# A graph network kernel: all 79 dense node tiles counted beside the first layer's gathers, and their stores begun by ScalarE

## Chip, cores and metric

The kernel runs on one core of one Trainium2 chip. The metric is the device time of one execution in microseconds (us), lower being better. The engines are TensorE (PE, its weight loads are PEld), VectorE (DVE), ScalarE (ACT), GpSimd (POOL) and SyncE (SP). Each runs its own instructions in order, and they wait for one another through semaphores.

## What is computed

There are 12500 nodes with 64 features and 400000 edges, sorted by target `dst`; `src` is random.

```
h = relu(layernorm(x))
m = silu(LN(concat(h[src], edge_attr) @ W1 + b1))       # first layer
m = silu(m @ W2 + b2)
x = x + LN(silu(concat(segment_sum(m, dst), h) @ Wu + bu))
h = relu(layernorm(x))                                   # second layer
agg = segment_sum(h[src], dst)
x = x + relu((h + agg) @ M1 + c1) @ M2 + c2
```

## The kernel before

**First layer.** The edges are cut into 391 blocks of 1024 (8 columns of 128). For every block POOL issues 8 indirect DMAs (`gather`, L736), each fetching 128 rows of 256 bytes by `src`. The block is then pushed through a pipeline written out by hand: one *step* per block, in which every engine does its part for blocks of different age. DVE adds the gathered rows to the edge products (`z_ready`, L1128), PE transposes and multiplies, ACT applies the activations, PE sums the messages of a block into a window of 40 nodes (`window_sums`, L781), and DVE adds the window to `cT`. Gathers run up to 4 blocks ahead of DVE (`AHEAD`).

**Second layer.** Its messages are only `h[src]`, so the sum for a tile of 128 target nodes is also a dense product: a matrix of counts (128 targets by 12500 sources) times `h`, which lies in SBUF as three bf16 parts (`hparts`). A tile's product is 100 matmuls of 125x192 (`product`, L1762), followed by a copy of the sums on ACT (L1715) and a turn of 3 float32 matmuls on PE (`turn`, L1773). The edges of 76 tiles go this way; the first 92 blocks of edges are still gathered, as in the first layer but with no MLP.

**Where the counts come from.** Of the 76 tiles, 48 are *stored*: their counts are made during the first layer's steps, and go through HBM (`ctab`, 128 x 12800 bf16 = 3.28 MB a tile, 400 KB a unit). A tile is 8 *units*, and in the code before step j does one unit: DVE compares keys with numbers in PSUM (`count_hots`, L1176 and L1178), PE multiplies the one-hots in two halves (`pairs`, L984, 16 matmuls in all), ACT copies each half out of PSUM (`staged`, L1057), and SP starts the store (L934). A tile also needs one indirect DMA of its keys on POOL (L949). The other 28 tiles are *built* in the second layer itself, beside the products of the other tiles (`one_hot_pairs` L1839 and L1841 on DVE, L1783 on PE, L1723 on ACT); their keys are fetched and masked while the nodes are updated between the layers (L1415 on POOL, L1571 and L1575 on DVE). A table of slots sets that order: 8 parts for a stored tile, 16 for a built one, and a block of gathered edges every 9 parts.

The program's parts in order: setup, first layer, node update, second layer, and the final MLP over 25 batches of 500 nodes (L1896, L1904, L1912), each stage behind a barrier of all engines.

## Time and profile before

| what | value |
|---|---|
| median of 3 runs | 5619.12 us (5618.64, 5619.12, 5668.9) |
| profiled execution | 5674.2 us, span 5672.3 us |
| setup, until the first gather | 198.8 us |
| first layer, gathers | 198.8 to 4162 |
| its pipeline running empty | to 4220 |
| node update | 4221 to 4384 |
| second layer | 4387 to 5505.9 |
| final MLP | 5505.9 to 5672 |
| busy: PE, DVE, ACT, POOL | 68%, 48%, 37%, 70% |

The profiled execution is one run, 55 us above the median of the others. Busy shares are means over stages with different limits, so each stage has to be read by itself.

### The profile page before, as it was taken

How to read it: one execution, taken by the hardware profiler on the slowest of the kernel's cores; microseconds unless marked ns; L12 is line 12 of the kernel's file. 1: busy time of each engine (PE TensorE's matmuls, PEld its weight loads, DVE VectorE, ACT ScalarE, POOL GpSimd, SP SyncE). 2: the span in 40 equal slices, each digit the busy share in tenths (PEclk: the TensorE clock that was granted, in tenths of full speed). 3: DMA queues.
4: the chain of work that ended last, by engine and by line, in shares of the span. 5: the costliest groups of instructions: out<-in, count | busy, mean ns of one | idle time of the engine just before them, and what ended most of it. 6: DMA issues, size and time to landing. Idle time of an engine off the chain costs nothing. (4 is left out here: it accounts for less than half of the span.)

```text
span 5672.3 us, 77979 instructions
## 1 busy us (share of the span) xinstructions
PE 3874.2 (68%) x27143; PEld 2832.3 (50%) x27143; DVE 2750.7 (48%) x5342; ACT 2073.5 (37%) x3073; POOL 3997.2 (70%) x4016
## 2 busy tenths in 40 slices
PE   5456666666666656666666666666675989989888
PEld 4334444443444434334444443444453888888873
DVE  5445555545454545454555555555557434434331
ACT  1133333333333343334333333333333333334332
POOL 3777777777777777777777777777732777777750
PEclk9567777777787787877778777778775999999995
DMA  3122222222222222222222222222212444444431
GB/s 94 49 72 83 80 78 82 79 81 81 81 81 79 80 81 80 81 80 80 81 80 81 80 80 81 80 81 80 81 43 72 143 183 157 167 176 159 176 122 31
DMA packets 324626, 529.74 MB, mean 93 GB/s; under 512 B 153682, under 2 KB 204114, under 8 KB 317586
## 3 DMA queue, kind: packets, MB, share of 16 engines
q1 hardware_dynamic: 198162, 395.39, 19.4%
q0 software_dynamic: 126080, 129.36, 10.0%
q8 instruction: 225, 3.69, 0.3%
q14 instruction: 159, 1.30, 0.1%
HBM read 352.75 MB, written 171.69 MB: 92 GB/s over the span
## 5 line engine op out<-in xcount | busy, mean ns | idle before, releaser
L736 POOL DMA_INDIRECT gat<-layer_rows,idx x3864 | 3820.1, 989 | 1181.5 <-issue 1175.1
L1057 ACT ACTIVATE node_buffers<-ps 128x800 bf16<-128x800 f32 x768 | 642.8, 837 | 2371.4 <-PE ps L984 2371.4
L781 PE MATMUL ps<-one_hots,edge_buffers 128*128 128x80 f32 x3128 | 602.0, 355 | 1092.4 <-DVE cT L828 1092.2
L1128 DVE TENSOR_TENSOR edge_buffers<-ps,gat 128x512 f32<-128x512 f32 x391 | 270.3, 691 | 1808.7 <-issue 1532.0
L781 PEld LDWEIGHTS ps<-one_hots,edge_buffers 128*128 128x128 f32 x3128 | 541.1, 261 | 1145.9 <-issue 1135.4
L1762 PE MATMUL ps<-edge_buffers,node_buffers 125*128 125x192 bf16 x7600 | 742.5, 252 | 18.2 <-DMA node_buffers<-stored_counts 12.4
L749 PE MATMUL ps<-w1e,edge_buffers 128*128 128x256 f32 x1564 | 633.7, 547 | 107.7 <-DVE edge_buffers L1128 103.7
L1762 PEld LDWEIGHTS ps<-edge_buffers,node_buffers 125*128 125x128 bf16 x7600 | 687.8, 141 | 36.8 <-DMA node_buffers<-stored_counts 15.8
L762 PE MATMUL ps<-edge_buffers,w2d 128*128 128x512 f32 x782 | 501.4, 728 | 0.7 <-ACT node_buffers L772 0.6
L1723 ACT ACTIVATE node_buffers<-ps 125x800 bf16<-125x800 f32 x448 | 371.2, 839 | 316.6 <-PE ps L1783 292.4
L1176 DVE TENSOR_TENSOR node_buffers<-ps,node_buffers 128x1024 bf16<-128x1024 f32 x384 | 469.5, 1223 | 15.2 <-PE ps L984 5.2
L767 PE MATMUL ps<-ident,node_buffers 128*128 128x128 f32 x1564 | 285.2, 312 | 276.5 <-ACT edge_buffers L776 276.5
L749 PEld LDWEIGHTS ps<-w1e,edge_buffers 128*128 128x128 f32 x1564 | 387.8, 274 | 164.5 <-issue 110.5
L984 PEld LDWEIGHTS ps<-node_buffers 64*128 64x128 bf16 x6144 | 185.7, 106 | 557.6 <-issue 529.8
L767 PEld LDWEIGHTS ps<-ident,node_buffers 128*128 128x128 f32 x1564 | 190.4, 158 | 378.6 <-issue 378.5
L1178 DVE TENSOR_TENSOR node_buffers<-ps,node_buffers 128x800 bf16<-128x800 f32 x384 | 376.3, 980 | 0.0
L756 PE MATMUL ps<-ident,node_buffers 128*128 128x128 f32 x1564 | 331.2, 348 | 5.0 <-ACT edge_buffers L1075 4.9
L824 DVE TENSOR_TENSOR cT<-cT,ps 64x40 f32 x483 | 88.9, 184 | 480.3 <-PE ps L781 367.5
L984 PE MATMUL ps<-node_buffers 64*128 64x100 bf16 x6144 | 320.1, 234 | 0.0
L1075 ACT ACTIVATE edge_buffers<-ps,gcol 128x512 f32<-128x512 f32 x391 | 302.1, 773 | 14.0 <-PE ps L756 14.0
L772 ACT ACTIVATE node_buffers<-ps,b2col 128x512 f32<-128x512 f32 x391 | 270.4, 692 | 0.8 <-PE ps L762 0.5
L1150 DVE TENSOR_TENSOR node_buffers<-edge_buffers,ps 128x512 f32<-128x512 f32 x391 | 265.5, 679 | 3.6 <-DVE ps L294 0.3
(201 smaller groups left out, 4031.0 us busy)
## 6 DMA issues: line engine op xcount, KB each, us to landing
stored_counts<-node_buffers SPq DMA_DIRECT2D x384, 400.0 KB, 2.4
node_buffers<-stored_counts SPq DMA_DIRECT2D x48, 3200.0 KB
gat<-layer_rows,idx POOLq DMA_INDIRECT x3864
edge_buffers<-in_edge_quads SPq DMA_DIRECT2D x391, 128.0 KB, 2.0
node_buffers<-in_x SPq DMA_DIRECT2D x5, 625.0 KB
layer_rows<-node_buffers SPq DMA_DIRECT2D x25, 125.0 KB
residual_rows<-node_buffers SPq DMA_DIRECT2D x5, 625.0 KB
layer_rows<-node_buffers SPq DMA_DIRECT2D x5, 625.0 KB
```

The lines of the kernel that those rows point to most:

```text
L736: pool.indirect_dma_start(out=gat[:, j, c, :], out_offset=None, in_=table[:, :], in_offset=bass.IndirectOffsetOnAxis(ap=idx[:, half, j, c: ...
L749: mm = pe.matmul(o[:, k * 4 * F:(k + 1) * 4 * F], ea[:, j, k, :], w1e[:, :], start=True, stop=True)
L756: mm = pe.transpose(o[:, k * 128:(k + 1) * 128], zn[:, j, 2 * k:2 * k + 2, :].rearrange("p c f -> p (c f)"), ident[:, :])
L762: return pe.matmul(mp[0][:, 0:PAIRS * 128], w2d[:, :], hT[:, j, :], start=True, stop=True)
L767: mm = pe.transpose(mp[1][:, k * 128:(k + 1) * 128], msgT[:, half, k * 128:(k + 1) * 128], ident[:, :])
L781: mm = pe.matmul(to[:, 0:2 * WIN], rows_of[:, 2 * k:2 * k + 2, :].rearrange("p c f -> p (c f)"), oh[:, j, 2 * k:2 * k + 2, :].rearrange("p ...
L984: mm = pe.matmul(tp[h][:, i * T:(i + 1) * T], low_hot[node, u % 2, k, :], high_hot[node, u % 2, k, :], start=True, stop=True)
L1057: a.activation(stage[:, u % STAGES, part * GP * T:(part + 1) * GP * T].rearrange("p (i h k) -> p h i k", h=2, k=T), ps[:, 2:4, 0:4 * T].re ...
L1176: v.tensor_tensor(low_hot[:, u % 2, :, :], per_tile(low_numbers, GP), bcast(low_key[:, b % 2, at], 128), ALU.is_equal).then_inc(c_low, 1)
L1178: v.tensor_tensor(high_hot[:, u % 2, :, :], per_tile(high_numbers, GP), bcast(high_key[:, b % 2, at], T), ALU.is_equal).then_inc(c_hot, 1)
L1723: a.activation(cnt[0:TP, d % 2, ch * 8 * T:(ch + 1) * 8 * T].rearrange("p (b k) -> p b k", b=2), built[ch % 2][0:TP, :, :], ACT.Copy).then ...
L1762: mm = pe.matmul(wide[d % 2], cnt[0:TP, d % 2, t:t + (GW - 1) * T + 1:T], hparts[:, t, :, :].rearrange("p k f -> p (k f)"), start=(t == 0) ...
```

## The change

Every dense tile is now stored, 79 of them, and none is built in the second layer; 78 blocks are gathered there in place of 92. The first layer makes 13 units in 8 steps (`RATE`) instead of 8, so 5 of 8 steps hold two units. The one-hot buffers go from 2 to 4 (`PAIR_SLOTS`). ACT starts each store itself (`write_counts`), after a wait for its own two copies. In the second layer each slot is one tile and, in 78 of 79, one block; three count buffers are loaded in turn, the first while the nodes are updated.

```diff
-    STORED, BUILT = 48, 28
-    TILES = STORED + BUILT
+    TILES = 79
...
-    GB = 92
+    GB = 78
+    RATE = (13, 8)
...
-        UNITS = STORED * GPS
-        FETCH, MASK, KEYS_TURN, HOTS, COUNT, STORE = 0, 4, 6, GPS, GPS + 1, GPS + 6
+        UNITS = TILES * GPS
+        FETCH, MASK, KEYS_TURN, HOTS, COUNT = 0, 4, 6, 8, 9
+        unit_step = [u * RATE[1] // RATE[0] for u in range(UNITS)]
...
-                    u = unit_at(e, j, STORE)
-                    if u is not None:
-                        at = u % GPS * 2 * GP * T
-                        wait(sp, c_copy, 2 * u + 2)
-                        sp.dma_start(ctab[u // GPS, :, at:at + 2 * GP * T], stage[:, u % STAGES, :]).then_inc(c_st[u % STAGES], 16)
...
+                def write_counts(u):
+
+                    at = u % GPS * 2 * GP * T
+                    wait(a, c_copy, 2 * u + 2)
+                    a.dma_start(ctab[u // GPS, :, at:at + 2 * GP * T], stage[:, u % STAGES, :]).then_inc(c_st[u % STAGES], 16)
...
+                    for u in units[0:1]:
+                        write_counts(u)
+                    for u in units[1:2]:
+                        staged(u, 0)
+                        staged(u, 1)
+                        write_counts(u)
...
-                    wait(v, c_use, 2 * (u - 2) + 2)
+                    wait(v, c_use, 2 * (u - PAIR_SLOTS) + 2)
...
+        def load_counts(sp, d):
+
+            sp.dma_start(cnt[d % 3], ctab[d, :, :]).then_inc(d_load[d % 3], 16)
...
+                    for d in range(1, TILES):
+
+                        wait(sp, d_sum, d - 2)
+                        load_counts(sp, d)
...
+                    for d in range(TILES):
+                        product(d, 0, LEAD)
+                        if d > 0:
+                            turn(d - 1)
+                        product(d, LEAD, T)
+                        if d < GB:
+                            sums(d)
```

The line numbers of the code after differ a little: `window_sums` is L775, `edge_products` L743, the transposes L750 and L761, the second product L756, `product` L1668, `turn` L1679.

On PE, a step of the first layer before, from the window sums to the second half of its unit (L984):

```order
L781 MATMUL ps<-one_hots,edge_buffers 128x80 x4
L749 MATMUL ps<-w1e,edge_buffers 128x256 x2
L984 MATMUL ps<-node_buffers 128x100 x8
L756 MATMUL ps<-ident,node_buffers 128x128 x4
L767 MATMUL ps<-ident,node_buffers 128x128 x4
L762 MATMUL ps<-edge_buffers,w2d 128x512
L984 MATMUL ps<-node_buffers 128x100 x8
```

and a step that holds two units after:

```order
L775 MATMUL ps<-one_hots,edge_buffers 128x80 x4
L743 MATMUL ps<-w1e,edge_buffers 128x256 x2
L984 MATMUL ps<-node_buffers 128x100 x8
L750 MATMUL ps<-ident,node_buffers 128x128 x4
L984 MATMUL ps<-node_buffers 128x100 x8
L761 MATMUL ps<-ident,node_buffers 128x128 x4
L984 MATMUL ps<-node_buffers 128x100 x8
L756 MATMUL ps<-edge_buffers,w2d 128x512
L984 MATMUL ps<-node_buffers 128x100 x8
```

The second half moved ahead of the back transposes, and a second unit's halves lie around the second product.

On ACT, a step of the first layer before, with what each instruction waits for (activation, first copy of counts, messages, messages by feature, second copy):

```order
L1075 ACTIVATE edge_buffers<-ps,gcol 128x512 [waits l0_second_products,l0_z_transposed]
L1057 ACTIVATE node_buffers<-ps 128x2x4x100 [waits stored_counts_written1,stored_pairs_multiplied]
L776 ACTIVATE edge_buffers<-ps 128x512 [waits l0_window_summed,l0_messages_turned]
L772 ACTIVATE node_buffers<-ps,b2col 128x512 [waits l0_messages_turned,l0_second_products]
L1057 ACTIVATE node_buffers<-ps 128x2x4x100 [waits stored_counts_written1,stored_pairs_multiplied]
```

and a step with two units after:

```order
L1085 ACTIVATE edge_buffers<-ps,gcol 128x512 [waits l0_second_products,l0_z_transposed]
L1061 ACTIVATE node_buffers<-ps 128x2x4x100 [waits stored_counts_written0,stored_pairs_multiplied]
L770 ACTIVATE edge_buffers<-ps 128x512 [waits l0_window_summed,l0_messages_turned]
L1061 ACTIVATE node_buffers<-ps 128x2x4x100 [waits stored_counts_written0,stored_pairs_multiplied]
L766 ACTIVATE node_buffers<-ps,b2col 128x512 [waits l0_messages_turned,l0_second_products]
L1068 DMA stored_counts<-node_buffers 128x1600 [waits stored_counts_staged]
L1061 ACTIVATE node_buffers<-ps 128x2x4x100 [waits stored_counts_written1,stored_pairs_multiplied] x2
L1068 DMA stored_counts<-node_buffers 128x1600 [waits stored_counts_staged]
```

ACT gained two stores, each behind a wait for its own copies, and the second unit's two copies in a row.

On PE in the second layer before, where a tile is built (L1783) between pieces of another tile's product, around the window sums of a block:

```order
L1783 MATMUL ps<-node_buffers 128x200 x4
L1762 MATMUL ps<-edge_buffers,node_buffers 128x192 x8
L1783 MATMUL ps<-node_buffers 128x200 x4
L781 MATMUL ps<-one_hots,gat 128x80 x4
L1762 MATMUL ps<-edge_buffers,node_buffers 128x192 x7
```

and after, the same row of work from one slot into the next:

```order
L1668 MATMUL ps<-edge_buffers,node_buffers 128x192 x75
L775 MATMUL ps<-one_hots,gat 128x80 x4
L1668 MATMUL ps<-edge_buffers,node_buffers 128x192 x25
L1679 MATMUL ps<-ident,node_buffers 64x128 x3
L1668 MATMUL ps<-edge_buffers,node_buffers 128x192 x75
```

The pairs are gone; the product is cut once, for the turn of the tile before.

## Rows read from the trace of the kernel before

**Rows 1.** Busy time by stretch: first layer, second layer, final MLP.

```profile
core 0: us, PE busy (x) PEld busy (x) DVE busy (x) ACT busy (x) POOL busy (x), PEclk, DMA share, GB/s
1000.00:4000.00 3000.00, 1878.90 (x11386) 1226.08 (x11385) 1547.76 (x3108) 1162.16 (x1702) 2267.46 (x2404) 0.79 0.27 80
4387.00:5505.00 1118.00, 1003.91 (x10584) 960.74 (x10584) 442.05 (x800) 400.09 (x614) 868.66 (x736) 0.95 0.45 164
5540.00:5580.00 40.00, 33.83 (x94) 14.52 (x94) 5.01 (x12) 10.97 (x18) 0.00 (x0) 0.50 0.17 38
```

**Rows 2.** Waits, 1000 to 4000 us: total, times, longest.

```profile
ACT node_buffers L1057 <- PE ps L984: 1826.4, 588, 10.2
DVE edge_buffers L1128 <- issue: 1168.6, 230, 7.7
PE ps L781 <- DVE cT L828: 865.3, 262, 7.5
```

**Rows 3.** Groups of instructions, 1000 to 4000 us: count, busy, mean ns, idle before.

```profile
L736 POOL DMA_INDIRECT gat<-layer_rows,idx x2367 | 2233.3, 944 | 721.4 <-issue 721.4
L1057 ACT ACTIVATE node_buffers<-ps 128x800 bf16<-128x800 f32 x592 | 495.5, 837 | 1826.5 <-PE ps L984 1826.4
L1176 DVE TENSOR_TENSOR node_buffers<-ps,node_buffers 128x1024 bf16<-128x1024 f32 x296 | 361.9, 1223 | 9.2 <-PE ps L984 1.2 <-issue 1.0
L1178 DVE TENSOR_TENSOR node_buffers<-ps,node_buffers 128x800 bf16<-128x800 f32 x296 | 290.0, 980 | 0.0
```

**Rows 4.** Timeline of the emptying pipeline: start, duration; two steps with units, two without.

```profile
4175.45 0.97 PEld L781 LDWEIGHTS ps<-one_hots,edge_buffers 128*128 128x128 f32 x8
...
4180.32 0.97 PEld L781 LDWEIGHTS ps<-one_hots,edge_buffers 128*128 128x128 f32 x8
...
4199.34 1.14 PEld L781 LDWEIGHTS ps<-one_hots,edge_buffers 128*128 128x128 f32 x8 [0.39 <-issue]
...
4201.91 1.15 PEld L781 LDWEIGHTS ps<-one_hots,edge_buffers 128*128 128x128 f32 x8 [0.38 <-issue]
```

**Rows 5.** Timeline of the node update: DVE's first wait, and its masking of keys.

```profile
4237.64 1.49 DVE L1543 TENSOR_REDUCE stat<-node_buffers 125x20 f32<-125x1280 f32 x1 [10.54 <-ACT node_buffers L1481]
...
4267.52 0.59 DVE L1575 TENSOR_TENSOR gat<-gat,node_buffers 128x384 bf16<-128x384 bf16 x1
```

**Rows 6.** Groups of instructions, second layer: the gathers.

```profile
L736 POOL DMA_INDIRECT gat<-layer_rows,idx x736 | 868.7, 1180 | 228.2 <-issue 221.8 <-ACT idx L804 5.2 <-PE ps L781 1.2
```

**Rows 7.** Timeline, second layer: gathers beside DVE and beside a load; product around a turn.

```profile
4600.63 1.67 POOL L736 DMA_INDIRECT gat<-layer_rows,idx  x1 [0.30 <-issue]
...
4608.78 2.09 PEld L1762 LDWEIGHTS ps<-edge_buffers,node_buffers 125*128 125x128 bf16 x25 [0.45 <-ACT node_buffers L1723]
...
4611.79 3.08 PEld L1762 LDWEIGHTS ps<-edge_buffers,node_buffers 125*128 125x128 bf16 x37 [0.17 <-issue]
...
4615.72 0.94 POOL L736 DMA_INDIRECT gat<-layer_rows,idx  x1 [0.30 <-issue]
```

**Rows 8.** Timeline, second layer: window sums of a block, and what follows on PE.

```profile
4413.47 0.97 PEld L781 LDWEIGHTS ps<-one_hots,gat 128*128 128x128 f32 x8
...
4414.32 0.67 PEld L1762 LDWEIGHTS ps<-edge_buffers,node_buffers 125*128 125x128 bf16 x7
```

**Rows 9.** Busy time by stretch, while counts are loaded: DMA share and GB/s last.

```profile
4463.00:4468.00 5.00, 2.51 (x13) 2.51 (x14) 0.00 (x0) 0.36 (x2) 3.78 (x5) 0.74 1.00 356
4614.00:4616.00 2.00, 1.06 (x13) 0.87 (x11) 0.00 (x0) 0.00 (x0) 1.39 (x3) 1.00 1.03 439
```

**Rows 10.** Timeline, second layer: a load, a gather issued during it, and PE's wait.

```profile
5476.71 0.32 SPq L1701 DMA_DIRECT2D node_buffers<-stored_counts  x1
...
5479.31 0.94 POOL L736 DMA_INDIRECT gat<-layer_rows,idx  x1 [0.30 <-issue]
...
5488.63 1.16 PEld L781 LDWEIGHTS ps<-one_hots,gat 128*128 128x128 f32 x8 [4.53 <-DMA gat<-layer_rows,idx]
```

**Rows 11.** Timeline, early in the final MLP.

```profile
5511.09 1.11 PE L1896 MATMUL ps<-cT,m 64*128 64x500 f32 x4
```

**Rows 12.** The chain of work that ended last, in the final MLP.

```profile
5521.53 2.04 PE ps L1896 x4
```

More of the change, by code:

```diff
@@ L1016, in step @@
                         transposes(pe, s, zp[1]).then_inc(g_t, 1)
+                    for u in units[0:1]:
+                        pairs(u, 1)
                     s, n = lagged(e, j, BACK)
@@ L1028, in step @@
                         second_products(pe, s).then_inc(g_m, 1)
-                    if u is not None:
+                    for u in units[1:2]:
                         pairs(u, 1)
@@ L1076, in step @@
                                      bias=gcol[:, 1:2], scale=gcol[:, 0:1]).then_inc(g_h, 1)
-                    u = unit_at(e, j, COUNT)
-                    if u is not None:
+                    units = units_at(e, j, COUNT)
+                    for u in units[0:1]:
                         staged(u, 0)
@@ L1085, in step @@
                         messages(a, s).then_inc(g_msg, 1)
+                    for u in units[0:1]:
+                        staged(u, 1)
                     s, n = lagged(e, j, FEAT)
@@ L1185, in step @@
                         mask(b)
-                    u = unit_at(e, j, HOTS)
-                    if u is not None:
+                    for u in units_at(e, j, HOTS):
                         wait(v, g_num, 3)
@@ L1422, in _ @@
                         low_part(g - 2)
-                    for k in range(len(batches_of_tiles[g])):
-                        node_edges(g, k)
                 low_part(CHUNKS - 2)
@@ L1613, in _ @@
             def _(sp):
+                with sp.If(flagged(sp) == 0):
+                    load_counts(sp, 0)
                 for k in range(2):
@@ L1649, in build_gnn @@
         d_add = sem("tile_sums_added")
-        built = [ps[:, 2 * k:2 * k + 2, 0:4 * T] for k in range(2)]
         wide = [ps[:, k, 0:3 * F] for k in (4, 7)]
@@ L1696, in _ @@
                 with sp.If(flagged(sp) == 0):
-                    for d in range(TILES):
-                        if not is_built[d]:
-                            wait(sp, d_sum, d - 1)
-                            sp.dma_start(cnt[:, d % 2, :], ctab[number[d], :, :]).then_inc(d_load[d % 2], 16)
+                    for d in range(1, TILES):
+                        wait(sp, d_sum, d - 2)
+                        load_counts(sp, d)
             @block.scalar
@@ L1715, in raw_sums @@
                     a.activation(raw[:, :], wide[d % 2], ACT.Copy).then_inc(d_raw, 1)
-                def counts(d, ch):
-                    wait(a, d_use, number[d] * CHS + ch + 1)
-                    if ch == 0:
-                        wait(a, d_sum, d - 1)
-                    a.activation(cnt[0:TP, d % 2, ch * 8 * T:(ch + 1) * 8 * T].rearrange("p (b k) -> p b k", b=2),
-                                 built[ch % 2][0:TP, :, :], ACT.Copy).then_inc(d_copy, 1)
-                def slot(d):
-                    for c in range(parts_of_slot[d]):
-                        at = slot_from[d] + c
-                        if d < TILES and is_built[d]:
-                            counts(d, c)
-                        if c == 0 and d > 1:
-                            raw_sums(d - 2)
-                        if at - 1 in sums_at and sums_at[at - 1] + UN < GB:
-                            index(sums_at[at - 1] + UN)
                 with a.If(flagged(a) == 0):
@@ L1737, in _ @@
                         index(n)
-                    for d in range(TILES + 1):
-                        slot(d)
-                    raw_sums(TILES - 1)
+                    for d in range(TILES):
+                        raw_sums(d)
+                        if d + UN < GB:
+                            index(d + UN)
             @block.tensor
```

216 lines of the change are left out of this document (51 added, 165 removed).

## Prediction

> **What bounds the kernel now.** I read the busy times by stretch first, then the waits and groups of the first layer, then the timeline of the second. In the first layer POOL issued 2404 indirect DMAs in 3000 us, one every 1.248 us, while PE, DVE and ACT were busy 1879, 1548 and 1162 us [rows 1]. A gather is 944 ns with 0.30 us of issue behind it, and its group shows no other idle time: POOL never waits for anyone [rows 3]. The others wait for it: DVE stood 1169 us before `z_ready` for what the profile calls issue, which is gathered rows that have not landed; PE's window sums waited 865 us for DVE, and ACT's copies 1826 us for PE [rows 2]. A step takes 8.125 POOL instructions (8 gathers and an eighth of a key fetch), 10.14 us. So in a step PE has 6.35 us of work, DVE 5.23, ACT 3.93, and the rest is slack.
>
> In the second layer the reader should look at POOL again, not only at the PE that is 90% busy. Its 736 gathers fill the stage, but now at 1180 ns and 0.30 us, 1.48 us each [rows 6]; 92 blocks at 8 x 1.484 us are 1092 of the 1118 us. The timeline shows why they are longer: 1.67 us where the bf16 compares L1839 and L1841 of a built tile run, 0.94 us beside a load of counts and no compare [rows 7].
>
> The final MLP ran at a granted clock of 0.50 [rows 1], with 2.04 us for a group of matmuls that took 1.11 us a few batches earlier [rows 11, 12].
>
> **The change, part by part.**
>
> *First layer, POOL.* 31 more key fetches at 1.25 us (a gather's price [rows 3]; a fetch has the same form). POOL sets the pace, so all of it counts: **+39 us**. A step becomes 8.20 instructions, 10.24 us.
>
> *First layer, the other engines.* Each step has 0.625 unit more on average. DVE: 1.22 + 0.98 us a unit [rows 3], +1.4 us, to 6.6 of 10.24. ACT: two copies of 0.84, +1.05 us, and for every one of 1.6 units a store to start, with a wait for its own last copy before it. The trace has no store started by ACT. SP's took 0.32 us [rows 10]; with nothing it is 0, and with 0.2 us more for the hand-over from its own copy (an estimate, half of the 0.45 us that PE shows behind a copy [rows 7]) 0.5 us. I take 0.5, so ACT comes to 5.8 of 10.24. What is queued behind that wait is the next copy, for which PE waits. PE: a unit's two halves are 0.8 us of matmuls, but they use one pair of PSUM banks, so half k+1 waits until ACT has copied half k (0.84 us and two hand-overs). The first unit's halves have the transposes between them; around the second unit only 0.6 to 1.1 us of other work lies between. I take 1.9 us for a second unit, 1.2 a step, and its upper bound is 3.3 (two full copies, two halves and hand-overs). PE then needs 7.6 to 8.4 of 10.24 us. All three stay under the POOL pace, and gathers run 4 blocks ahead, so a step of 11 us is repaid by the next: **0**. Without this cover it would be 1.2 us times 391 steps, 470 us. SP loses its stores and delays nobody with or without them: 0.
>
> *The pipeline running empty.* Here no gather hides anything. Units now go on until count step 397 in place of 392; about 10 more units lie behind the last gather. A step there took 4.87 us with a unit and 2.57 without [rows 4], 2.3 us a unit: **+20 us** (10 to 30).
>
> *Node update.* 28 fetches, five maskings (0.59 and 0.55 us on DVE [rows 5]), their turns and copies go. DVE is nearly always busy there and POOL is not: **-6 us**. The load of tile 0 is put ahead of two small loads on SP's queue that DVE needs early. It takes about 8 us, and DVE has 10.5 us of idle time just there [rows 5]: 0, at worst +3.
>
> *Second layer.* Three engines come close together now, so each needs a price per slot (a tile and a block). PE: weight loads pace the product at 83 ns each (25 in 2.09 us, 37 in 3.08), 8.3 us for 100; from the end of the 25 to the 37 behind the turn are 0.9 us [rows 7]; the window sums take 0.85 [rows 8]; with a hand-over 10.2 us, all at the full clock. POOL: 8 gathers of 1.248 us, 9.98 us, because no bf16 compare is left. DMA: 3.28 MB and 0.26 MB of gathers are 8.1 us at the 439 GB/s of the best stretch with the queues full and 9.9 at the 356 of the worst [rows 9]. So PE paces it, at 10.2 us. The pace rests on gathers that land late without hurting: the one issued at 5479.3, during a load, let PE go on only at 5488.6 [rows 10], 8 us later, but four blocks may be under way, 40 us. At the start two loads are queued at once and PE waits for block 0, some 18 us in. Then 77 slots of 10.2 are 785 us, and the last window sums, the last product, its copy, turn and addition 13 us. Some stretches at half clock behind a wait add perhaps 1.5%, 12 us. Sum 828 us against 1119 (the 1118 of the row [rows 1] and the hand-over into the MLP): **-291 us**, with 800 at POOL's pace and 895 with PE at 10.7 us and an uneven start as ends.
>
> At this place the Trainium skill has a rule on the gathers (SBUF — State Buffer, the section on doors and the "DVE blocks DMA" trap): a DMA issued from GpSimd has its descriptors written there, and a DVE instruction in a two-port mode locks it out. [...] If gathers were slow for another reason, the sum would be that of the second rival.
>
> *Sum.* 5674.2 + 39 + 20 - 6 - 291 = 5436 us for an execution like the profiled one. The median of the runs is 55 us lower, and I read that as the MLP's clock: its batches hold three groups of matmuls, each nearly twice as long at 0.50, some 2.3 us for 22 batches or more, 50 us. Two of three runs had it fast, so I take the same for the median after: 5619.1 - 238 = **5381 us**. At half clock there, 5432.
>
> **The rivals.**
>
> *First rival, transfers bound the second layer.* With one load under way at a time and two microseconds between issue and full rate, the 9.9 us of the slow stretch becomes 11.8 a slot, 78 x 1.6 = 125 us more: 5506. For it: 347 GB/s would be needed throughout, and the stage before had 164 [rows 1]. Against: three buffers let the next load be queued before the last has landed, and the full-rate stretch had 439 GB/s. The Trainium skill (DMA: Bandwidth & Descriptors, Specifications) gives about 358 GB/s as what HBM yields one core, by which a slot's transfers would be 9.9 us, still under PE's 10.2; the 439 GB/s of the trace is above it.
>
> *Second rival, gathers stay slow*, so the change doesn't free them: at 1.484 us, 78 blocks are 926 us, with start and end 955: 5508. For it: they were slow in just the stage with the loads. Against: the 0.94 us beside a load [rows 7].
>
> *Third rival, slower.* The first layer's step leaves POOL's pace. The mechanism is a ring: DVE's `count_hots` waits for PE's last halves, those for ACT's copies, ACT is held by its own store waits, and DVE's next window additions, on which PE's step starts, stand behind `count_hots`. If PE's step is 11 us and DVE's part behind it 7 to 10, two steps take as much as the 20.5 us that POOL gives them. It decides from 10.85 us a step, where 0.61 x 391 eats the 238 us. At 11.3 it costs 415 us: 5796. For it: half of PE's time in that stage is at half clock or near (mean 0.79 [rows 1]), and all figures above are from rows where much of it was fast. Against: 4 blocks of lead and 2 to 4 us of slack on each engine.
>
> **How the numbers follow.** The forecast gets 0.74 (the MLP fast 0.5, slow 0.24), the first rival 0.09, the second 0.06, the third 0.05, and 0.06 is for things between, such as a first layer slower by 0.3 us a step (5500). The range is 5335 (POOL's pace in the second layer, nothing lost at the emptying) to 5500 (an uneven second layer and the slow MLP, or most of the small first-layer loss). A measurement of this kernel can tell about 1%, 56 us: faster by more 0.94, within 0.02, slower 0.04.
>
> **What would show it.** After, POOL's gathers should be 944 ns in both layers with 0.30 us between them in the first; the first layer's last gather should come 39 us later, at about 4200; the second layer should last about 830 us, PE busy over 95% at a clock near 1, and POOL should show waits for PE's window sums. A first layer in which POOL waits for DVE makes the third rival right; a second layer in which PE waits for counts or rows, with a DMA share near 1, the first; gathers over 1.1 us the second. The prediction is wrong in size if slots are not near 10.2 us.

## The result, and the profile after

| | before | after |
|---|---|---|
| median of the runs, us | 5644.01 (4 runs, 5618.64 to 5670.93) | 5363.43 (4 runs, 5358.88 to 5368.85) |
| ratio, 95% interval | | 0.9503 [0.9441, 0.9564] |
| profiled execution, us | 5674.2 | 5365.3 (span 5363.6) |

The forecast was 5381 us, in a range from 5335 to 5500. The runs before fall into two pairs, near 5619 and near 5670 us, the four after into one. Against the lower pair alone the change saves 255 us, 0.955 times. From here on all times of stages are those of the two profiled executions:

| stage | before | after | difference | forecast |
|---|---|---|---|---|
| first layer, last gather issued at | 4160.9 | 4200.3 | +39 | +39 |
| from there to the node update | 60.8 | 86.8 | +26 | +20 |
| node update | 164.9 | 156.4 | -8.5 | -6 |
| second layer | 1119.3 | 813.1 | -306 | -291 |
| final MLP | 166.4 | 107.1 | -59 | 0, or about -50 with the faster clock |

Busy times by stretch after, which answer to [rows 1] (columns as there), for a part of the first layer, of the second layer and of the final MLP:

```profile
1000.00:4000.00 3000.00, 1961.58 (x14276) 1274.86 (x14276) 1914.55 (x3490) 1460.26 (x2092) 2267.61 (x2404) 0.81 0.34 105
4500.00:5200.00 700.00, 700.00 (x7916) 679.88 (x7915) 74.53 (x278) 37.19 (x138) 530.64 (x556) 1.00 0.92 353
5300.00:5363.00 63.00, 45.82 (x244) 21.96 (x240) 12.12 (x29) 26.05 (x43) 0.00 (x0) 0.98 0.19 42
```

In the first layer POOL still issues 2404 indirect DMAs in 3000 us, the same number as before, while DVE does 24% more work (1914.6 for 1547.8) and ACT 26% more. In the second layer PE is busy for every one of the 700 us, at a granted clock of 1.00.

The groups of the first layer, 1000 to 4000 us, answer to [rows 3]: count, busy, mean ns, idle before.

```profile
L730 POOL DMA_INDIRECT gat<-layer_rows,idx x2345 | 2212.8, 944 | 714.7 <-issue 712.3 <-PE ps L995 1.8 <-DVE edge_buffers L1144 0.6
L1061 ACT ACTIVATE node_buffers<-ps 128x800 bf16<-128x800 f32 x950 | 795.1, 837 | 1421.8 <-PE ps L984 1399.1 <-issue 10.1
```

POOL waited 2.4 us for others in 3000; ACT still waits 1399 us for PE, where it waited 1826 [rows 2]. The added work went into waiting time.

The groups of the second layer, 4410 to 5260 us, answer to [rows 6]:

```profile
L730 POOL DMA_INDIRECT gat<-layer_rows,idx x624 | 596.4, 956 | 192.1 <-issue 189.9 <-ACT idx L798 2.2
L775 PE MATMUL ps<-one_hots,gat 128*128 128x80 f32 x624 | 82.3, 275 | 9.7 <-DMA gat<-layer_rows,idx 9.7
```

The gather takes 956 ns and not 1180, and PE waited for gathered rows once, 9.7 us for block 0. The timeline of one slot, from window sums to window sums:

```profile
5232.97 0.97 PEld L775 LDWEIGHTS ps<-one_hots,gat 128*128 128x128 f32 x8
...
5233.82 2.15 PEld L1668 LDWEIGHTS ps<-edge_buffers,node_buffers 125*128 125x128 bf16 x25
...
5236.08 0.63 PEld L1679 LDWEIGHTS ps<-ident,node_buffers 128*64 128x64 f32 x6
...
5236.88 6.22 PEld L1668 LDWEIGHTS ps<-edge_buffers,node_buffers 125*128 125x128 bf16 x75 [0.17 <-issue]
...
5243.04 0.97 PEld L775 LDWEIGHTS ps<-one_hots,gat 128*128 128x128 f32 x8
```

5243.04 less 5232.97 is 10.07 us a slot: the window sums 0.85, 25 weight loads 2.15 and 0.11 behind them, the turn 0.63 and 0.17 behind it, and 6.16 from the first of the 75 loads to the next window sums.

POOL has no slack there either: in its group above the idle time is 0.30 us of issue behind each gather and 2.2 us once. Its slot is the same, because one gather in eight runs beside DVE's compare for the one-hots of a block (L785) and is longer:

```profile
4854.07 0.48 DVE L785 TENSOR_TENSOR one_hots<-winf,rel_all 128x320 f32<-128x320 bf16 x1
4854.35 1.01 POOL L730 DMA_INDIRECT gat<-layer_rows,idx  x1 [0.30 <-issue]
4855.67 0.94 POOL L730 DMA_INDIRECT gat<-layer_rows,idx  x1 [0.31 <-issue]
```

From 4445 to 5230 us the 73 gathers that overlap L785 alone of DVE's instructions take 1038 ns in the mean, and all others but one 944. The last gather of a block ends 12.1 us before PE's window sums of that block, for block 3 as for block 70. PE, busy all the time, sets this pace, but POOL without L785 beside it would need 9.99 us, so at most 0.1 us a slot could be gained on PE before POOL sets the pace.

The emptying pipeline in the timeline, to hold against [rows 4]:

```profile
4207.93 0.97 PEld L775 LDWEIGHTS ps<-one_hots,edge_buffers 128*128 128x128 f32 x8 [1.10 <-issue]
...
4214.60 0.97 PEld L775 LDWEIGHTS ps<-one_hots,edge_buffers 128*128 128x128 f32 x8 [1.12 <-issue]
...
4221.56 1.78 PEld L775 LDWEIGHTS ps<-one_hots,edge_buffers 128*128 128x128 f32 x8
...
4229.81 0.34 PEld L775 LDWEIGHTS ps<-one_hots,edge_buffers 128*128 128x128 f32 x1 [0.52 <-issue]
...
4230.66 1.62 PEld L775 LDWEIGHTS ps<-one_hots,edge_buffers 128*128 128x128 f32 x7 [0.52 <-issue]
...
4238.50 1.78 PEld L775 LDWEIGHTS ps<-one_hots,edge_buffers 128*128 128x128 f32 x8
...
4261.54 0.97 PEld L775 LDWEIGHTS ps<-one_hots,edge_buffers 128*128 128x128 f32 x8
```

The five steps from 4221.56 to 4261.54 take 8.0 us each, the one from 4207.93 6.67 us. The granted clock was 0.50 there, as the busy times of a part of it show, and the weight loads took 1.78 us where they took 0.97:

```profile
4239.00:4250.00 11.00, 10.91 (x72) 7.29 (x72) 7.18 (x14) 7.43 (x11) 0.00 (x0) 0.50 0.29 113
```

And the chain of work that ended last, in the final MLP, where [rows 12] had 2.04 us for the first of these groups:

```profile
5266.21 1.11 PE ps L1760 x4
5267.32 0.99 PE ps L1768 x4
5268.31 1.03 PE ps L1776 x8
```

### The profile page after: what moved, and what is told of

Read it like the earlier page. It is cut to its first block and busy times, and to the rows that moved or that the text cites. A ratio compares the mean times of both kernels' runs of the same rounds, so it can differ in the third digit from the quotient of the medians.

```text
span 5363.6 us, 84119 instructions
## 1 busy us (share of the span) xinstructions
PE 3756.4 (70%) x29537; PEld 2707.8 (50%) x29537; DVE 2902.7 (54%) x5403; ACT 2133.7 (40%) x3162; POOL 3723.8 (69%) x3907
## 5 line engine op out<-in xcount | busy, mean ns | idle before, releaser
L730 POOL DMA_INDIRECT gat<-layer_rows,idx x3752 | 3548.2, 946 | 1145.5 <-issue 1140.5
L1061 ACT ACTIVATE node_buffers<-ps 128x800 bf16<-128x800 f32 x1264 | 1057.9, 837 | 1878.2 <-PE ps L984 1849.1
L775 PE MATMUL ps<-one_hots,edge_buffers 128*128 128x80 f32 x3128 | 603.9, 356 | 886.7 <-DVE cT L822 886.4
L775 PEld LDWEIGHTS ps<-one_hots,edge_buffers 128*128 128x128 f32 x3128 | 540.4, 260 | 1029.2 <-issue 1018.2
L1192 DVE TENSOR_TENSOR node_buffers<-ps,node_buffers 128x1024 bf16<-128x1024 f32 x632 | 770.2, 1219 | 9.6 <-issue 0.7
L743 PE MATMUL ps<-w1e,edge_buffers 128*128 128x256 f32 x1564 | 642.9, 554 | 97.4 <-DVE edge_buffers L1144 93.5
L1668 PE MATMUL ps<-edge_buffers,node_buffers 125*128 125x192 bf16 x7900 | 686.0, 247 | 6.0 <-PEq L1407 6.0
L1668 PEld LDWEIGHTS ps<-edge_buffers,node_buffers 125*128 125x128 bf16 x7900 | 665.4, 139 | 19.8 <-issue 19.8
L984 PEld LDWEIGHTS ps<-node_buffers 64*128 64x128 bf16 x10112 | 304.3, 101 | 695.3 <-issue 643.1
L1194 DVE TENSOR_TENSOR node_buffers<-ps,node_buffers 128x800 bf16<-128x800 f32 x632 | 619.0, 979 | 0.0
L984 PE MATMUL ps<-node_buffers 64*128 64x100 bf16 x10112 | 494.5, 222 | 158.4 <-ACT node_buffers L1061 97.7
L756 PE MATMUL ps<-edge_buffers,w2d 128*128 128x512 f32 x782 | 462.4, 675 | 182.9 <-ACT node_buffers L766 181.0
L743 PEld LDWEIGHTS ps<-w1e,edge_buffers 128*128 128x128 f32 x1564 | 395.5, 279 | 157.4 <-issue 101.6
L750 PE MATMUL ps<-ident,node_buffers 128*128 128x128 f32 x1564 | 305.7, 327 | 23.5 <-ACT edge_buffers L1085 22.4
L761 PE MATMUL ps<-ident,node_buffers 128*128 128x128 f32 x1564 | 266.2, 297 | 41.4
L756 PEld LDWEIGHTS ps<-edge_buffers,w2d 128*128 128x128 f32 x782 | 120.6, 194 | 244.8 <-issue 244.8
```

Source lines behind the costliest of these rows:

```text
L730: pool.indirect_dma_start(out=gat[:, j, c, :], out_offset=None, in_=table[:, :], in_offset=bass.IndirectOffsetOnAxis(ap=idx[:, half, j, c: ...
L743: mm = pe.matmul(o[:, k * 4 * F:(k + 1) * 4 * F], ea[:, j, k, :], w1e[:, :], start=True, stop=True)
L750: mm = pe.transpose(o[:, k * 128:(k + 1) * 128], zn[:, j, 2 * k:2 * k + 2, :].rearrange("p c f -> p (c f)"), ident[:, :])
L756: return pe.matmul(mp[0][:, 0:PAIRS * 128], w2d[:, :], hT[:, j, :], start=True, stop=True)
L775: mm = pe.matmul(to[:, 0:2 * WIN], rows_of[:, 2 * k:2 * k + 2, :].rearrange("p c f -> p (c f)"), oh[:, j, 2 * k:2 * k + 2, :].rearrange("p ...
L984: mm = pe.matmul(tp[h][:, i * T:(i + 1) * T], low_hot[node, u % PAIR_SLOTS, k, :], high_hot[node, u % PAIR_SLOTS, k, :], start=True, stop= ...
```

## The experiments

They ran in three later sessions, on three chips (13, 9 and 10), and in all three **the unchanged kernel before took 7428 to 7737 us** instead of 5619 to 5671. For the first two traces and their runs, called the first session here, no chip is on record; it may have been one of the three. So the difference is one between sessions, and whether the chip makes it is not shown, though the expectations speak of chips. Totals that an expectation takes from the first session could not come out later, and each run is read stage by stage. This is all of them, totals and ratios from the medians of the runs and the rest from the profiled executions, with the two first traces on top. "Emptying" runs from the last gather of the first layer to the node update, the second layer from its first gather to the first matmul of the final MLP, "gather" is the mean of the second layer's.

| run | chip | total, us | ratio to before in that session | step, first layer | emptying | second layer | gather, ns |
|---|---|---|---|---|---|---|---|
| before, first trace | - | 5644 | 1 | 10.13 | 61 | 1119 | 1180 |
| after, first trace | - | 5363 | 0.950 | 10.23 | 87 | 813 | 956 |
| before again (b1) | 9 | 7428 | 1 | 14.02 | 81 | 1384 | 1144 |
| before, short compares (b2) | 9 | 7603 | 1.018 [1.012, 1.025] | 14.16 | 83 | 1495 | 954 |
| after, three loads (e6) | 9 | 7959 | 1.067 [1.063, 1.072] | 15.75 | 115 | 1219 | 949 |
| after, compares (e5) | 9 | 7812 | 1.049 [1.043, 1.055] | 15.72 | 114 | 1091 | 1152 |
| after again (a1) | 10 | 8056 | 1.050 [1.044, 1.056] | 15.97 | 117 | 1226 | 953 |
| after, SyncE stores (e7) | 10 | 8047 | 1.050 [1.043, 1.057] | 15.96 | 107 | 1218 | 953 |
| after, quarter products (a2) | 10 | 7768 | 1.013 [1.007, 1.019] | 15.15 | 118 | 1219 | 954 |
| after, SyncE stores (e1) | 13 | 7906 | 1.059 [1.054, 1.064] | 15.74 | 108 | 1179 | 953 |
| after, two a step (e2) | 13 | 7951 | 1.065 [1.061, 1.069] | 15.98 | 69 | 1175 | 954 |
| after, 5 in 3 steps (e3) | 13 | 7983 | 1.071 [1.066, 1.075] | 16.02 | 79 | 1153 | 960 |
| after, two slots (e4) | 13 | 8402 | 1.126 [1.122, 1.131] | 16.96 | 130 | 1167 | 956 |

Durations of instructions are those of the first traces (a gather 946 to 954 ns, a copy of counts 0.84 us); what grew is waiting. The ratios are to the kernel before in the same session, with a median of 7 runs each: 7452.96, 7685.84 and 7462.67 us on chips 9, 10 and 13.

### Both kernels again, nothing edited

> The kernel before, unchanged, for one more profile. Theory (its runs of 5619 and of 5670 us differ by TensorE's clock in the final MLP): a run of 5619 shows the final MLP in about 107 us at a granted clock near 1 there, one of 5670 shows 166 us at 0.50, and all other stages the same within 5 us. Rival: the 50 us lie in the layers, and the MLP takes 166 us in either.

> The changed kernel, nothing edited, beside the kernel before on the same chip. The runs so far stood on chips where the kernel before took 7428 to 7496 us and not 5619 to 5671. There its trace counts 14.0 us a step of the first layer where the first trace has 10.3, and PE's increments of semaphores reach the waiting engines up to 25 us after the matmul that carries them, while POOL stands idle. Theory: the forecast rests on the gathers' pace of 1.25 us being the first layer's bound; on such a chip it is not the bound, so each unit of counting that is put beside the gathers lengthens the step. The five variants of the changed kernel there had 15.7 to 16.0 us a step with four pair slots. This theory expects 7850 to 7980 us here (first layer 6150 to 6250, second 1050 to 1170), slower than before by about 6 per cent, if the kernel before is again near 7450; and 5360 to 5375 us against about 5640 if the chip is like the first one. Rival: it was the edits of the variants that cost the time, and the changed kernel unedited gains here too, about 7100 us (7450 less the 310 to 370 us that the second layer loses).

Measured: 7427.5 us for the kernel before (one run), 8055.7 for the changed one, which is 1.050 [1.044, 1.056] times the kernel before beside it. **The change that saved 5% in the first session costs 5% in this one.** It does so unedited, so the slower totals of the variants did not come from their edits. Its total is 76 us above the upper end expected, on a chip where the kernel before is also some 230 us slower than on the other two. (The 10.3 us a step that the expectation has for the first trace of before is 10.13 in the table.)

The expectation for the kernel before asked about its final MLP. It took 110 us at a granted clock of 0.94, like the 107 us after, but in a run that is slow everywhere else. That the pairs of 5619 and 5670 us differ by this stage stays an inference from the profiled run near 5670, whose MLP took 166 us at 0.50.

The busy times from 1000 to 4000 us, of the kernel before again:

```profile
1000.00:4000.00 3000.00, 1391.71 (x8110) 886.34 (x8110) 1103.10 (x2212) 823.43 (x1211) 1622.21 (x1716) 0.69 0.21 57
```

and of the changed kernel again:

```profile
1000.00:4000.00 3000.00, 1359.26 (x9039) 869.13 (x9038) 1208.77 (x2201) 928.39 (x1324) 1440.16 (x1523) 0.65 0.22 66
```

POOL issued 1716 and 1523 indirect DMAs where it issued 2404 in both first traces. It no longer sets the pace. The waits of the kernel before again, same stretch (total, times, longest), say so directly:

```profile
ACT node_buffers L1057 <- remote: 1533.1, 139, 23.5
...
POOL gat L736 <- DVE edge_buffers L1128: 757.1, 93, 10.6
```

POOL waits for DVE's `z_ready`, and ACT waits up to 23.5 us for something that the profile can't name. The timeline shows what it is, here in the kernel before again:

```profile
2003.52 0.52 PE L984 MATMUL ps<-node_buffers 64*128 64x100 bf16 x8
...
2005.76 1.99 PE L749 MATMUL ps<-w1e,edge_buffers 128*128 128x256 f32 x4
...
2007.61 0.94 POOL L736 DMA_INDIRECT gat<-layer_rows,idx  x1 [0.30 <-issue]
2012.76 0.84 ACT L1057 ACTIVATE node_buffers<-ps 128x800 bf16<-128x800 f32 x1 [11.53 <-remote]
2012.86 1.23 DVE L1176 TENSOR_TENSOR node_buffers<-ps,node_buffers 128x1024 bf16<-128x1024 f32 x1 [20.96 <-remote]
```

ACT's copy needs the half that PE's L984 made, which by its record was over at 2004.04; it starts 8.7 us later, and DVE, which waits for the same, with it. The trace's records of semaphore increments agree: those of four different groups of PE's matmuls, whose ends lie from 2001.9 to 2006, all arrive from 2012.60 to 2012.83. I counted the increments from 1000 to 4000 us against the end of the last matmul that could have made them. In the first trace of before, none of 2104 of PE's came over 1 us late; here 42% of 1322 did, the latest by 25.5 us, and in the changed kernel again 30% of 1437, the latest by 37.7. Of ACT's and DVE's increments from 1000 to 4000 us none is late in any trace. The ends of matmuls are modelled in these profiles, so this is a comparison with a model; but ACT and DVE start only when the increments arrive.

What follows: in these sessions a step is a loop of hand-overs through PE (PE, ACT's copy, PE's next half, DVE's next compare), each held up at times, and no gather hides it. The difference by stages on one chip, chip 9, where b1 and e6 stood (e6 leaves the first layer of the changed kernel alone): the first layer of the change, with 0.625 unit more a step, another order on PE, ACT's stores and four slots, costs 1.73 us a step, 1.73 x 391 = 676 us, and 34 us more in the emptying; the node update gives back 11, the second layer 165, the MLP 4. That is 530 us, and 7959 less 7428 is 531. It says where the time goes, not which part of the change costs it.

### Who starts the stores

SyncE starts them again, as before the change, and ScalarE has neither the stores nor the waits before them.

```diff
+                    for u in units_at(e, j, STORE):
+                        at = u % GPS * 2 * GP * T
+                        wait(sp, c_copy, 2 * u + 2)
+                        sp.dma_start(ctab[u // GPS, :, at:at + 2 * GP * T], stage[:, u % STAGES, :]).then_inc(c_st[u % STAGES], 16)
...
-                    for u in units[0:1]:
-                        write_counts(u)
                     for u in units[1:2]:
                         staged(u, 0)
                         staged(u, 1)
-                        write_counts(u)
```

> The changed kernel with one part undone: SP starts the 632 stores again, 13 steps after a unit's keys, and ACT has neither the stores nor the waits before them. Theory: ACT's part of a step (4.98 us busy of 10.24) is under POOL's pace, so the first layer's gathers end at the same time within 2 us; only where the pipeline runs empty may 1 to 4 us be saved. About 5361 us, the same as the changed kernel's 5363. Rival (starting the stores on ACT costs ACT time that matters, or the SP queue holds up edge loads): different by over 15 us, faster if ACT's waits cost, slower if SP, waiting for copies, brings edge rows too late.

> The changed kernel with the stores of counts begun by SyncE again (the same file as the run that took 7906 us), now on the same chip as the unedited changed kernel. Theory: which engine begins a store costs nothing on the path, 0.33 us of ScalarE's queue a store beside 5.8 of 10.24 us; so the ratio to the unedited changed kernel is 0.99 to 1.01 in the total and the first layer's step differs by less than 0.1 us. Rival: ScalarE's stores are a part of the change's effect, by over 1 per cent in either direction: worse, since ScalarE is a link of the chain in the first layer, or better, since SyncE's loads of edge rows are no longer queued behind a store that waits for a copy; then the step differs by over 0.15 us.

Measured: 1.059 [1.054, 1.064] times before on chip 13; on chip 10, beside the unedited changed kernel, 8046.67 us against 8055.7. The step is 15.96 us against 15.97. In the steps ScalarE's stores cost nothing, as the first theory says. The 9 us between the medians are within the scatter of the runs (8035 to 8109). In the emptying 10 us stand between them, and the busy times of that stage, first of the unedited kernel and then of this one, show what they go with:

```profile
6449.00:6566.00 117.00, 87.20 (x648) 57.35 (x648) 66.97 (x131) 67.67 (x97) 0.57 (x1) 0.78 0.21 75
6444.00:6551.00 107.00, 76.57 (x660) 50.78 (x660) 66.38 (x130) 67.82 (x98) 0.95 (x1) 0.90 0.24 83
```

PE is busy 10.6 us longer at a lower granted clock, 0.78 against 0.90, while ACT is busy as long in both. The runs with SyncE's stores have 107 and 108 us, those with ScalarE's and the same units 114 to 118, so the difference recurs; how the stores move the clock is not shown.

### PE's part of the added work

PE makes 4 of the 16 matmuls of each unit, so the stored tables are not the counts.

```diff
-                    for i in range(4):
+                    for i in range(1):
```

> The changed kernel, in which PE makes 4 of the 16 matmuls of each unit of counting beside the gathers; the tables are then not the counts, and every wait, copy, compare, fetch and store stays. Theory A: on a chip where PE's increments come late the lateness goes with PE's work, so 12 of the some 40 matmuls a step fewer shorten the step from 15.7 us by 1 us or more, total below 7500 us. Theory B: it goes with the number of waits and increments that pass between PE and the others, which stay; then the step stays within 0.3 us of the unedited kernel's and the total within 120 us. On a chip like the first both give 10.24 us a step and a total within 0.3 per cent of the changed kernel, since POOL's gathers set the pace there and PE is busy 7.6 to 8.4 us of each step.

Measured: 7768.33 us, 1.013 [1.007, 1.019] times before and 287 us less than the unedited kernel; the step is 15.15 us, 0.82 less, 320 us in the whole first layer. That is between the two theories: too much for B's 0.3 us, short of A's 1 us. Twelve matmuls less in each of 1.625 units are 19.5 a step, so a matmul of 100 columns is worth 42 ns there. By that price the 10 matmuls in 0.625 unit are 0.4 of the 1.73 us; the rest is not the matmuls themselves.

### The ring's slack: two one-hot slots in place of four

```diff
-    PAIR_SLOTS = 4
+    PAIR_SLOTS = 2
```

> The changed kernel with one part undone: 2 one-hot buffers (PAIR_SLOTS 2) in place of 4. DVE then writes a unit's one-hots only when PE is done with the unit two before, often one of the step just before, and stands in front of its next z_ready with that wait. Theory (steps have 2 to 4 us of slack and gathers a lead of 4 blocks): DVE waits show up, some 1 us a step, but POOL keeps the pace, so 5363 to 5375 us. Rival (the ring DVE, PE, ACT closes over one step): steps above 10.24 us, 0.3 to 1 us each, 5480 to 5750 us.

Measured: 1.126 [1.122, 1.131] times before, the step 16.96 us against 15.74 of e1 on the same chip (e1 has SyncE's stores, which leave the step alone). So the two added slots are worth 1.22 us a step there, 477 us. With two slots DVE's `count_hots` waits for the halves of two units before, not four, by which late increments of PE would reach DVE sooner; that is argued. What the slots are worth where POOL sets the pace, which is what the expectation was about, was not measured.

### The rate: fewer or no units behind the last gather

```diff
-    RATE = (13, 8)
+    RATE = (2, 1)
```

In the second run it is (5, 3).

> The changed kernel with two units in every step (RATE 2,1) in place of 13 in 8 steps, so that the tiles are done at step 325 of 391. It doubles down on the load of PE, DVE and ACT while it lasts. Theory (POOL paces, 10.24 us a step, and a step with two units needs about 9 us of PE): the gathers of the first layer still end at about 4200 us within 3 us, and the emptying of the pipeline falls back from 87 to about 61 us, so about 5338 us. A step with two units then still shows POOL gathers 0.30 us apart. Rival (third rival of the prediction, the ring of DVE, PE and ACT binds at two units a step): steps of 11 us or more while the units last, 316 x 0.75 = 240 us or more later, 5580 us.

> The changed kernel with 5 units in 3 steps (RATE 5,3), 632 units done at step 379 + 9 = 388, just before the last gather. Theory (the units behind the last gather cost 2.3 us each at the emptying, 26 us in the changed kernel): the emptying is shorter by 20 to 26 us and nothing else changes: about 5340 us. Rival (the emptying is long for another reason, such as the clock of 0.50 there): within 8 us of 5363.

Measured: 1.065 [1.061, 1.069] and 1.071 [1.066, 1.075]. At two units a step all are done before the last gather, and the emptying is 69 us against the 108 of e1 on that chip; at 5 in 3 it is 79. Against the 114 to 117 us of the changed kernel with ScalarE's stores, which these two keep, it is 45 to 48 and 35 to 38 us less. That confirms what the +20 of the forecast was made of: units that have no gather beside them. But the first layer grew by 94 and 110 us against e1, and the totals are 45 and 77 us above e1's. That two units in a row stretch a step that no gather hides would explain it; no run tests that. Where POOL sets the pace the first effect should stay and the second not; that is argued, not measured.

### Are DVE's compares what makes a gather long?

The kernel before with its compares cut to 4 of 128 and of 200 numbers from the third group on, so that it leaves out most built counts (the work of all other instructions stays):

```diff
+                    nl, nh = (128, 2 * T) if b * GPS + g < 2 else (4, 4)
...
```

> The kernel before with DVE's one-hot compares of the built tiles cut to 4 of 128 and of 200 columns (after the first two groups), so this leaves out most of that DVE work and the counts of the built tiles; all of PE's, ACT's and POOL's work stays. Theory (POOL paced the second layer there, because of these compares): gathers fall from 1180 to about 960 ns, POOL needs 92 x 10.1 = 930 us, and PE, 1004 us busy, takes over as the bound: second layer about 1020 to 1035 us in place of 1119, so 85 to 100 us off, about 5525 to 5590 according to the clock of the final MLP. Rival (PE bound it already): within 20 us of before.

The changed kernel with three pairs of the old compares added to each slot, on a buffer that nobody reads:

```diff
+                    for d in range(TILES):
+                        for k in range(3):
+                            compares(3 * d + k)
```

> The changed kernel with the suspected cost put back alone: in each of the 79 slots of the second layer DVE also makes three pairs of the bf16 compares (128x1024 and 128x1600) that a built tile needed, into a buffer that nobody reads. About as many per gathered block as before (2.4), no PE work with them. Theory (these compares hold up the writing of gather descriptors on POOL): gathers rise from 956 to about 1200 ns, POOL takes 8 x 1.5 = 12.0 us a block and paces the second layer: 78 x 12 = 936 and 20 more, 955 us in place of 813, about 5505 us in all. Rival (the gathers were slow before for another reason, the loads or their number): gathers stay at 0.95 us, the second layer at 813, 5363 us.

Measured: the gathers answer clearly, whatever the session does to the rest. Groups of the kernel before again, 6000 to 7200 us:

```profile
L736 POOL DMA_INDIRECT gat<-layer_rows,idx x659 | 761.3, 1155 | 439.7 <-ACT idx L804 239.8 <-issue 199.8
```

with the compares cut:

```profile
L1840 DVE TENSOR_TENSOR node_buffers<-iol,node_buffers 128x32 bf16<-128x32 bf16 x181 | 31.1, 172 | 419.9 <-PE ps L1783 224.0 <-remote 184.8 <-issue 11.2
...
L736 POOL DMA_INDIRECT gat<-layer_rows,idx x607 | 577.7, 952 | 617.4 <-ACT idx L804 435.4 <-issue 182.0
```

and of the changed kernel with compares added, 6800 to 7500 us:

```profile
L732 POOL DMA_INDIRECT gat<-layer_rows,idx x412 | 477.8, 1160 | 222.3 <-issue 118.6 <-ACT idx L800 101.9 <-PE ps L777 1.8
...
L1730 DVE TENSOR_TENSOR node_buffers<-ioh,identb 128x1600 bf16<-128x1600 bf16 x154 | 152.9, 993 | 5.3
```

Without the long compares 952 ns, with them 1155 to 1160, in either kernel. (The changed kernel without them has 949 ns in e6, on the same chip.) The stage did not follow: b2's second layer is 111 us longer than b1's though its gathers are 0.2 us shorter, and e5's is 128 us shorter than e6's though its gathers are 0.2 us longer. In these sessions gathers don't bound that stage, so b2 can't show that they did in the first session; that rests on [rows 6], where 92 blocks of such gathers fill 1092 of 1118 us. Less work on DVE goes with a longer stage in both pairs, and I have no cause for that.

### Do the loads of counts bound the second layer?

The changed kernel loads counts for three tiles only and multiplies those again and again, so its sums are of the wrong tiles:

```diff
-                    for d in range(1, TILES):
-
-                        wait(sp, d_sum, d - 2)
+                    for d in range(1, 3):
                         load_counts(sp, d)
...
-                        wait(pe, d_load[d % 3], 16 * (d // 3 + 1))
+                        wait(pe, d_load[d % 3], 16)
```

> The changed kernel with only the first 3 of the 79 tiles loaded; the products use them again and again, so this leaves out 76 loads and the counts of those tiles. Theory (PE paces the second layer at 10.1 us a slot, transfers are hidden): second layer 813 us less the uneven first 40 us, some 5 to 12 us; 5350 to 5360 in all, the slot stays 10.1 us. Rival (a DMA share of 0.92 slows matmuls or gathers): slots get shorter than 10 us or POOL's gathers faster, over 20 us gained, below 5343.

Measured: 1.067 [1.063, 1.072]. The busy times from 6800 to 7200 us of this kernel:

```profile
6800.00:7200.00 400.00, 330.90 (x3009) 306.00 (x3008) 28.50 (x106) 13.68 (x52) 199.17 (x211) 0.88 0.10 18
```

and of the changed kernel again, on chip 10:

```profile
6800.00:7200.00 400.00, 328.19 (x2962) 302.00 (x2960) 27.84 (x104) 13.92 (x52) 196.81 (x207) 0.87 0.61 228
```

With 18 GB/s in place of 228 PE gets through 3009 matmuls and not 2962, 1.6% more, and a gather takes 949 ns and not 953. The two ran in different sessions, so a difference this small need not come from the loads; the second layer takes 1219 and 1226 us. The loads neither bound the stage nor lengthen the gathers. This was measured at 228 GB/s, not at the 353 of the first session; there the timeline of the slot above has no wait for a load at all.

## Why the prediction was right, and where not

**First layer, +39.** Measured +39.1: 31 more instructions on POOL at 1.25 us each. That was right because POOL did not wait for anyone, which is one row [rows 3] before and one row after.

**The other engines at nothing.** Right in the first session. DVE has 6.53 us of work in a step (1914.55 of 3000, of 10.24), 6.6 was forecast; ACT 4.98, and 0.33 for each of 1.6 stores makes 5.5, forecast 5.8; PE 6.70 busy; its need with its waits, put at 7.6 to 8.4, is in no row. This is the step on which the sign hangs. The third rival had it as a ring whose step leaves POOL's pace, with a break-even at 10.85 us; in the three later sessions the ring takes 15.7 to 16.0 us, POOL waits for DVE, and the change, unedited, costs 5% in the session in which it ran. The mechanism was the rival's, the reason was not: it named longer matmuls at half clock, and what the traces show there is PE's increments arriving late. The granted clock was lower too, 0.69 for 0.79 before and 0.65 for 0.81 after, but PE's busy time a step grew only from 6.35 to 6.50 us and from 6.70 to 7.24, while the steps grew by 3.9 and 5.7. The sentence "without this cover it would be 1.2 us times 391 steps" names the right kind of price, too low: 1.73 us a step was measured between b1 and e6.

**Emptying, +20.** Measured +26, inside the 10 to 30 given. The term was 10 units at 2.3 us (23, taken as 20); the size is off by the clock: five steps there took 8.0 us each at 0.50, 6.6 us more in all than at the 6.67 us of the step at the full clock, and the rows I took with a unit were at the full one [rows 4]. The clock of this stage is therefore a term that the sum lacked.

**Node update, -6.** Measured -8.5. The early load of tile 0 starts at 4287.67, ahead of the small ones, and did not lengthen the stage: DVE now waits 11.45 us for its small load, against 10.54 for ACT in [rows 5].

**Second layer, -291.** Measured -306. The slot is 10.07 us, 10.2 was forecast, and its parts agree (75 loads at 83 ns are 6.2, 25 in 2.15). The 15 us of difference: the 77 slots from 4464.32 to 5243.04 take 778.7 us where 785 were forecast, 6 less. The 12 us counted on top for stretches at half clock fall away; the 2.4 us of it that came are in the first slot, of 12.5 us, and so in the 778.7. Start and end were 21 and 13.5 us, forecast 18 and 13. That PE was busy all the time came as said. POOL's waits for PE's window sums, named as a sign of it, did not: POOL never waited for them. Its 9.98 us a slot were worked out with no bf16 compare left, but L785 is one, reading two bf16 inputs in SBUF, and one gather in eight takes 1038 ns beside it. So the two engines run level at 10.08 us, and the margin was thinner than forecast.

That the gathers shorten because the compares go was an argument from one timeline before; b2 and e5 now show it in both directions. The reason that the prediction gives, DVE in a two-port mode, is not shown. All that the rows have is that the compares which lengthen a gather (L1839, L1841, L785 in the second layer) are TENSOR_TENSOR with both inputs in SBUF, while the compares L1192 and L1194 and the same L785 in the first layer, with one input in PSUM, leave it at 944 ns. No run takes apart where the inputs lie, their type and the mode.

**First rival, transfers.** Out: PE never waited for a load, with a DMA share of 0.92 and 353 GB/s held for 700 us. The Trainium skill's figure (DMA: Bandwidth & Descriptors, Specifications) is about 358 GB/s from HBM to one core. The trace neither confirms nor contradicts it as a limit: 353 is about what the slots ask for (3.54 MB in 10.07 us are 352), and the stretch of 439 in [rows 9] is above it. **Second rival, slow gathers.** Out: 956 ns.

**The total.** 5363 against 5381: the second layer is 15 us under its term, the node update 2, the MLP 4 (59 us less where 55 were taken), the median 2 below the profiled execution, and the emptying 6 over. The ratio compares with a median before of 5644.0 and not 5619.1, since a fourth run of the kernel before took 5670.93; two of its four runs are near 5670, as the profiled one with the MLP at a clock of 0.50 was. Here the forecast was also lucky: it gave the fast MLP twice the chance of the slow one, on three runs. The change does not touch that stage, yet it makes 59 of the 309 us between the profiled executions, and why all four runs after had it fast and two of four before is not known.

So the forecast was right for the session that it was made for, and its chance of 0.04 for slower says nothing on the later ones: the same two programs differ there by as much in the other direction.

## What to carry to other kernels

- Work put beside a stage's pacing engine is free only as long as that engine really paces. One row shows it in the first layer, the pacing engine's idle time with no releaser but issue. In the second layer after, two engines have such a row, and what each would need alone (PE 10.07, POOL 9.99 us a slot) has to be worked out. The price without cover (here 1.7 us a step, 391 times) should stand beside the zero.
- An engine that issues its DMAs in software can be slowed by what another engine runs. If its instructions are 25% longer in one stage than in another, look for what runs beside them before counting them as that stage's cost.
- Time a schedule that leans on one engine's pace in more than one session, and on more than one chip, before keeping it. Here the margin between the ring and the gathers, 2 to 4 us a step, was gone in three of four.

## What the runs showed that I had not expected

- The same program took 5619 to 5671 us in the first session and 7428 to 7737 in three later ones, on three chips, with gathers, copies and compares of the same length. PE's increments came up to 25.5 us (37.7 in the changed kernel) behind its matmuls, none of ACT's or DVE's. The traces there also hold fewer records of increments, 31343 where the first holds 89794, with the same number of instructions. Both may have one cause, and whether recording a run is part of it can't be told from here. All runs of a kernel in such a session agree within 1.1%, so it is no disturbance that passes between runs. What makes PE late stays open.
- The lateness is not even over a run. By the same count the setup and the final MLP have none in any trace, and the MLP takes 106 to 110 us in all later runs but e2 (121), as in the first trace after (107). In the changed kernel again 29% of PE's increments are late while the first layer's gathers are issued, 3 of 29 in the 30 us behind the last one, none of 135 from there to the second layer, and 7% of 236 in the second layer. So late increments go with the stages in which POOL issues gathers; whether those cause them no run tests.
- In the second layer 353 GB/s were moved for 700 us while PE was busy all the time at the full clock, and the small gathers beside it kept their 956 ns.
